# Attention weights split in pieces, with their rest part on GpSimd, and a reordered start of both feed-forward phases

## The chip, the cores and the metric

The kernel runs on one core of one Trainium2 chip. A core has five engines with instruction queues of their own: TensorE (PE: matmuls and transposes into PSUM), VectorE (DVE), ScalarE (ACT), GpSimd (POOL) and SyncE (SP), which here only issues DMA transfers. Each queue is worked off in order; engines wait for each other on semaphores. Time is device time of one execution in microseconds (us), the median of several runs.

## The reference

x has 4 x 512 tokens of 256 values. All is fp32.

```python
x = x + 0.5 * ffn(layernorm(x))
x = x + attention(layernorm(x))      # 16 heads of 128, 4 key/value heads, rope, causal
x = x + 0.5 * ffn(layernorm(x))

def ffn(x):
    logits = x @ router_w + router_b                      # 8 experts
    topk_vals, topk_idx = top_k(logits, 2)
    full_w = one_hot sum of softmax(topk_vals)            # (tokens, 8)
    h = silu(einsum('td,edf->etf', x, expert_w) + expert_b[:, None, :])
    out = einsum('etf,te->tf', h, full_w) @ proj_w + proj_b
    y = x + out
    return norm_w * y / sqrt(mean(y * y) + 1e-6)
```

## The kernel before

Every fp32 matmul is made of three products of parts: an operand is copied by ScalarE into a rounded lead part (`hi`, type fp32r), and the rest part (`lo`) is the operand minus the lead. hi*hi, hi*lo and lo*hi are summed in PSUM. The two parts of the weights are made on the chip as well.

There are three phases: feed-forward f1 (0 to 168 us), attention (168 to 734 us), feed-forward f2 (734 to 867 us). `ffn_phase` makes both f1 (`first` is true) and f2. Every engine's instructions are written in order in a function of its own, with helpers and a `body(i)` for each of four blocks of 512 tokens. A block has 16 units (a pair of experts p = 0..3, half g = 0..1, tile t = 0..1): TensorE's `experts` makes a unit of 128 tokens x 2 experts in one of four PSUM banks (`ex`, used in a ring), ScalarE applies `silu` in place, VectorE's `weighted` adds it, times the router's weight, to `acc` and so frees the bank. Between the units lie the other steps: layer norm of a later block (`norm_stats`, `norm_rows` on VectorE, `rstd` on GpSimd; the rows `z` are transposed by TensorE, `z_lead` and `z_rest` split them), the router (`router`, `logits_out`, `logits_back`, `choose`, `half_tanh`, `weigh_chosen`), and the end of the block before (`sum_T`, `sum_lead`, `sum_rest`, `project`, `add_residual`, `squares`, `mean_square`, `inverse_rms`, `scale_rows`, `add_rows`). f1 also normalises blocks 0 and 1 again, for attention (j = 4 and 5 of `NORMS`).

f1 does more beside its blocks. The expert weights are shifted by a row (`row_of`, a K = 2 matmul of TensorE per pair of experts; `shift_pair` on VectorE for pairs 0 and 1; `row_out` on ScalarE and `shift_late` on GpSimd for pairs 2 and 3) and split (`pair_lead`, `pair_rest`). And the attention weights of four groups, in the order 1, 2, 3, 0, are loaded into `ga` (`a_raw`), their queries scaled by GpSimd (`scale_queries`), split into `gb` (`a_hi`) and `gc` (`a_lo`), and stored to `split` in DRAM, from which the attention phase reads them. Group 0 stays on the chip, in other buffers. A group is split in four pieces of 640 columns: `group_lead` on ScalarE and `group_rest` on VectorE, both at the places that `SLOTS` names (slot 8*i + 4*g + p of the order of units). SyncE's `store_group` waits until all four pieces of a group are split, then issues the load of the next group and two stores. `group_lead` waits for the scaling and, from the second group on, for the stores of the whole group before (semaphore `a_out`), as it overwrites `gb`:

```python
                    act.wait_ge(a_scaled, C * k + C)
                    if k > 0 and (ORDER[k] > 0 or m > 0):
                        act.wait_ge(a_out, 32 * k)
```

The kernel prints below with the line numbers of the profile: `group_lead` is line 623, `group_rest` 420, `silu` 602, `squares` 612, `weighted` 442 and 445, `norm_rows` 358, `pair_rest` 425, `scale_queries` 282, `residual` 265, `shift_late` 273, `row_of` 733, `router` 740 and 741, `experts` 764 to 766, `transpose_z` 719.

## Time and profile before

| | |
|---|---|
| time, median of 3 runs | 867.75 us (866.32 to 869.53) |
| the profiled execution | 870.1 us, its span 867.2 us |
| granted TensorE clock, mean | 0.971 |
| TensorE busy | 803.8 us (93% of the span) |
| VectorE busy | 679.8 us (78%) |
| ScalarE busy | 503.6 us (58%) |
| GpSimd busy | 484.8 us (56%) |
| HBM read and written | 19.77 MB and 11.01 MB, 35 GB/s over the span |

The span runs from the first to the last instruction; some time lies around it. A busy share is an average over three phases with different limits; the rows further below look at single stretches. In them L623 is line 623 of the kernel, "[5.98 <-DMA ...]" means that the engine stood idle for 5.98 us before this instruction and what released it, and PEclk is the clock granted to TensorE, as a share of full speed.

### The profile page before, as it was taken

What the parts mean: (1) busy time and instruction counts of PE and PEld (TensorE: products, weight loads), DVE (VectorE), ACT (ScalarE), POOL (GpSimd) and SP (SyncE); (2) the same over time, 40 slices, a digit from 0 to 9 for tenths busy, and PEclk for the clock granted to TensorE, in tenths of its full rate; (3) what the DMA queues carried; (4) which work ended last, traced back from release to release, by engine and by line L of the source; (5) the groups of instructions that cost most, each with busy time, mean ns of one, the idle gap of its engine ahead of it and who ended that gap; (6) DMA issues with size and microseconds to landing.
All of it is one profiled execution on the core that took longest, in us unless ns stands there. A gap on an engine that the chain in (4) does not pass through costs nothing. (4 is left out here: it accounts for less than half of the span.)

```text
span 867.2 us, 16033 instructions
## 1 busy us (share of the span) xinstructions
PE 803.8 (93%) x4712; PEld 703.5 (81%) x4712; DVE 679.8 (78%) x1948; ACT 503.6 (58%) x1241; POOL 484.8 (56%) x382
## 2 busy tenths in 40 slices
PE   7897897867899999999999999999999998799995
PEld 4676676655799999999998998999999997688884
DVE  6887898599966877868768768768778797888874
ACT  3434544445665766767758558657667674445442
POOL 4312331268577787777877877877877751212211
PEclk9998998979999999999999999999999999899997
DMA  9040451410112312312212212132121100000001
GB/s 306 3 173 16 176 183 48 115 44 13 37 30 69 97 24 48 83 38 73 73 36 58 75 36 73 24 97 49 56 65 30 40 17 1 1 1 25 25 1 49
DMA packets 25238, 52.18 MB, mean 60 GB/s; under 512 B 3442, under 2 KB 9202, under 8 KB 23922
## 3 DMA queue, kind: packets, MB, share of 16 engines
q1 hardware_dynamic: 25204, 51.77, 20.9%
q8 instruction: 16, 0.26, 0.1%
q14 instruction: 18, 0.15, 0.1%
HBM read 19.77 MB, written 11.01 MB: 35 GB/s over the span
## 5 line engine op out<-in xcount | busy, mean ns | idle before, releaser
L1147 DVE TENSOR_TENSOR at_ptl<-at_pt,at_pth 128x512 fp32r<-128x512 f32 (+1 forms) x192 | 108.8, 593 | 45.0 <-ACT at_pth L1293 44.9
L1293 ACT ACTIVATE at_pth<-at_pt 128x512 fp32r<-128x512 f32 (+1 forms) x192 | 94.2, 525 | 85.6 <-PE at_pt L1451 85.6
L1287 ACT ACTIVATE at_pr<-at_pr,at_low 128x512 f32<-128x512 f32 (+3 forms) x256 | 140.5, 557 | 2.3 <-DVE at_low L1133 2.2
L1035 POOL TENSOR_TENSOR at_ql<-at_rot,at_qh 128x512 fp32r<-128x512 f32 x62 | 79.7, 1285 | 98.1 <-ACT at_qh L1272 98.1
L602 ACT ACTIVATE f_ex<-f_ex 128x512 f32<-128x512 f32 x128 | 74.1, 583 | 86.4 <-PE f_ex L766 86.2
L445 DVE SCALAR_TENSOR_TENSOR f_acc<-f_ex,f_full,f_acc 128x256 f32<-128x256 f32 x224 | 95.9, 476 | 33.4 <-ACT f_ex L602 32.7
L1142 DVE TENSOR_SCALAR at_pr<-at_pr,at_inv 128x128 f32<-128x128 f32 (+3 forms) x256 | 110.5, 492 | 2.3
L1050 POOL TENSOR_TENSOR at_rot<-at_rot,gc 128x512 f32<-128x512 f32 x78 | 101.4, 1300 | 8.1 <-POOLq L1067 2.1
L1044 POOL TENSOR_TENSOR at_rot<-ga,cos 128x512 f32<-128x512 f32 x78 | 101.9, 1307 | 4.1 <-POOL at_ql L1035 2.4
L1451 PE MATMUL at_pt<-ident,at_pr 128*128 128x128 f32 x640 | 94.1, 278 | 9.5 <-DVE at_pr L1142 8.6
L1046 POOL TENSOR_TENSOR gc<-gc,sin 128x512 f32<-128x512 f32 x78 | 102.3, 1312 | 0.0
L764 PE MATMUL f_ex<-f_e_hi,zh 128*128 128x512 f32 x224 | 94.4, 421 | 6.5 <-DVE f_e_lo L425 4.4
L1133 DVE CUSTOM_DVE_ANT_0 at_pr<-at_sc,at_mask 128x512 f32<-128x512 f32 (+2 forms) x192 | 100.4, 546 | 0.0
L1272 ACT ACTIVATE at_qh<-at_rot 128x512 fp32r<-128x512 f32 x64 | 40.5, 633 | 92.7 <-POOL at_rot L1050 90.6
L765 PE MATMUL f_ex<-f_e_hi,zl 128*128 128x512 f32 x224 | 91.6, 409 | 0.0
L766 PE MATMUL f_ex<-f_e_lo,zh 128*128 128x512 f32 x224 | 91.1, 406 | 0.0
L1465 PE MATMUL at_o<-at_pth,at_vh 128*128 128x512 f32 (+3 forms) x256 | 82.7, 323 | 0.1
L1467 PE MATMUL at_o<-at_pth,at_vl 128*128 128x512 f32 (+3 forms) x256 | 82.4, 322 | 0.0
L1466 PE MATMUL at_o<-at_ptl,at_vh 128*128 128x512 f32 (+3 forms) x256 | 82.2, 321 | 0.0
L1451 PEld LDWEIGHTS at_pt<-ident,at_pr 128*128 128x128 f32 x640 | 71.2, 142 | 12.4 <-DVE at_pr L1142 9.7
L1440 PE MATMUL at_sc<-at_keys,at_ql 128*128 (+4 forms) x256 | 78.0, 316 | 0.0
L1438 PE MATMUL at_sc<-at_keys,at_qh 128*128 (+3 forms) x192 | 71.3, 371 | 5.4 <-DVE at_ql L1224 5.4
(212 smaller groups left out, 2130.8 us busy)
## 6 DMA issues: line engine op xcount, KB each, us to landing
gc<-ga SPq DMA_DIRECT2D x160, 128.0 KB, 2.3
ga<-in_attn_w SPq DMA_DIRECT2D x4, 1280.0 KB, 7.1
at_wo<-attn_split SPq DMA_DIRECT2D x8, 512.0 KB, 4.1
attn_split<-gb SPq DMA_DIRECT2D x3, 1280.0 KB, 9.8
attn_split<-gc SPq DMA_DIRECT2D x3, 1280.0 KB, 12.4
gb<-attn_split SPq DMA_DIRECT2D x6, 512.0 KB, 4.2
x<-in_x SPq DMA_DIRECT2D x4, 512.0 KB, 9.3
e_raw<-in_expert_w SPq DMA_DIRECT2D x8, 256.0 KB, 6.0
```

The costliest lines, as they stand in the source:

```text
L445: dve.scalar_tensor_tensor(out=acc[:, tile, :], in0=h, scalar=full_w[:, tile, e:e + 1], in1=acc[:, tile, :], op0=ALU.mult, op1=ALU.add).th ...
L764: pe.matmul(o, zh[:, c, tok], hi[:, :, w], start=(c == 0), stop=False)
L765: pe.matmul(o, zl[:, c, tok], hi[:, :, w], start=False, stop=False)
L1044: pool.tensor_tensor(rot[r % 2][:], raw[r], cosT[:], ALU.mult)
L1046: pool.tensor_tensor(swap[r], swap[r], sinT[:], ALU.mult).then_inc(sin_done, 1)
L1050: pool.tensor_tensor(rot[r % 2][:], rot[r % 2][:], swap[r], ALU.add).then_inc(sum_done, 1)
L1133: dve.tensor_tensor_reduce(out=out, in0=sc[bank][:, col:col + w], in1=masked, scale=1.0, scalar=3e38, op0=ALU.add, op1=ALU.min, accum_out= ...
L1142: dve.tensor_scalar(a, a, inv[h % 2][:, i:i + 1], None, ALU.mult).then_inc(nm_done, 1)
L1147: dve.tensor_tensor(ptl[h % 2][:, cols], pt[(NF * h + k) % 2][:, 0:FLEN[k]], pth[h % 2][:, cols].bitcast(F32), ALU.subtract).then_inc(lo_d ...
L1287: act.activation(pr[h % 2][:, cols], pr[h % 2][:, cols], ACT.Exp, bias=low[h % 2][:, i:i + 1], scale=-1.0, accum_out=tot[h % 2][:, i:i + 1 ...
L1293: act.activation(pth[h % 2][:, cols], pt[(NF * h + k) % 2][:, 0:FLEN[k]], ACT.Copy).then_inc(hi_done, 1)
L1451: r = pe.transpose(pt[(NF * h + k) % 2][:, col + (i - kt) * P:col + (i - kt + 1) * P], pr[h % 2][:, OFF[i] + kt * P:OFF[i] + (kt + 1) * P] ...
```

## The change

- A group of attention weights has its four pieces at the columns 0, 768, 1536, 2048 and 2560 (`EDGES`). Load, store and both semaphores (`a_in`, `a_out`) are per piece: SyncE stores a piece as soon as it is split, and then loads the same piece of the next group. `group_lead` waits for its own piece. The last group keeps its layout.
- `SLOTS` moves two pieces of groups 1, 2 and 3 one slot later.
- `group_rest` goes from VectorE to GpSimd, to fixed places in GpSimd's body: two pieces behind `residual` and two at the end.
- Start of f1: on VectorE `norm_rows(0)` comes ahead of `shift_pair(0)`, and `z_rest(0)` ahead of `pair_rest(0)`; the three small operations on constants move from VectorE to GpSimd, ahead of `shift_late`. On ScalarE `z_lead(0)` comes first, and `row_out(3)` behind `logits_out(0)`. On TensorE `row_of(2)` comes behind the first transposes, `row_of(3)` behind the router.
- Start of f2: `pair_rest(2)` comes ahead of `weigh_chosen(0)` (as it already does in f1), and GpSimd's `residual(0)` waits for it.

The diff, with parts that only rename or delete calls cut out:

```diff
--- before.py
+++ after.py
@@ -125,6 +125,10 @@
         w_ps = [ps(f"wide{n}", [P, SEQ]) for n in range(2)]
         t_ps = [ps(f"t{n}", [P, SEQ]) for n in range(2)]
 
+        ORDER = (1, 2, 3, 0)
+        EDGES = (0, QKV, C * QKV, C * QKV + G * D // 2, GW)
+        PIECES = len(EDGES) - 1
+
         rows_in, cols_in = (sem(n) for n in ("rows_in", "cols_in"))
         e_hi_done, e_lo_done, p_hi_done, p_split, r_split, setup, consts = (sem(n) for n in ("e_hi_done", "e_lo_done", "p_hi_done", "p_split", "r_split", "setup", "consts"))
         ln_stats, ln_aggr, ln_var, rstd_done, z_done = (sem(n) for n in ("ln_stats", "ln_aggr", "ln_var", "rstd_done", "z_done"))
@@ -139,7 +143,8 @@
         if first:
             e_in = [sem(f"e_in{n}") for n in range(PAIRS)]
             ident_in, x_in, e_row_in = sem("ident_in"), [sem(f"x_in{n}") for n in range(BATCH)], sem("e_row_in")
-            a_in, a_scaled, a_hi_done, a_lo_done, a_out, wa_in = (sem(n) for n in ("a_in", "a_scaled", "a_hi_done", "a_lo_done", "a_out", "wa_in"))
+            a_in, a_out = ([sem(f"{n}{m}") for m in range(PIECES)] for n in ("a_in", "a_out"))
+            a_scaled, a_hi_done, a_lo_done, wo_out = (sem(n) for n in ("a_scaled", "a_hi_done", "a_lo_done", "wo_out"))
             tables_in, step_done = sem("tables_in"), sem("step_done")
             row_ready, e_shifted, row_done, e_shifted_late = (sem(n) for n in ("row_ready", "e_shifted", "row_done", "e_shifted_late"))
 
@@ -154,9 +159,7 @@
         J0 = 0 if first else 1
         NORMS = BATCH + 2 if first else BATCH
 
-        ORDER = (1, 2, 3, 0)
-        PIECES = 4
-        SLOTS = ((3, 4, 5, 6), (10, 11, 12, 13), (17, 18, 19, 20), (25, 26, 27, 28))
+        SLOTS = ((3, 4, 5, 6), (9, 10, 12, 13), (17, 18, 20, 21), (25, 26, 28, 29))
 
         def piece_at(i, g, p):
 
...
-        def group_piece(i, m):
-
-            if ORDER[i] > 0:
-                part = slice(m * GW // PIECES, (m + 1) * GW // PIECES)
+        def group_piece(k, m):
+
+            if ORDER[k] > 0:
+                part = slice(EDGES[m], EDGES[m + 1])
...
@@ -196,14 +199,15 @@
         def _(sp):
             xr = d["x"].rearrange("(b t p) d -> b p t d", t=BT, p=P)
 
-            def load_group(i):
-                sp.dma_start(a_raw[:], d["attn_w"][ORDER[i]]).then_inc(a_in, 16)
-
-            def store_group(i):
-                sp.wait_ge(a_lo_done, PIECES * (i + 1))
-                load_group(i + 1)
-                sp.dma_start(split[ORDER[i], 0], a_hi[:].bitcast(F32)).then_inc(a_out, 16)
-                sp.dma_start(split[ORDER[i], 1], a_lo[:].bitcast(F32)).then_inc(a_out, 16)
+            def load_piece(k, m):
+                part = slice(EDGES[m], EDGES[m + 1])
+                sp.dma_start(a_raw[:, part], d["attn_w"][ORDER[k]][:, part]).then_inc(a_in[m], 16)
+
+            def store_piece(k, m):
+                part = slice(EDGES[m], EDGES[m + 1])
+                sp.wait_ge(a_lo_done, PIECES * k + m + 1)
+                sp.dma_start(split[ORDER[k], 0][:, part], a_hi[:, part].bitcast(F32)).then_inc(a_out[m], 16)
+                sp.dma_start(split[ORDER[k], 1][:, part], a_lo[:, part].bitcast(F32)).then_inc(a_out[m], 16)
 
             def load_block(b):
@@ -223,17 +227,22 @@
                 load_pair(2)
                 load_pair(3)
                 load_block(1)
-                load_group(0)
+                for m in range(PIECES):
+                    load_piece(0, m)
                 for b in range(2, BATCH):
                     load_block(b)
                 sp.dma_start(cosT[:], d["rope_cos"]).then_inc(tables_in, 16)
                 sp.dma_start(sinT[:], d["rope_sin"]).then_inc(tables_in, 16)
-                for i in range(KV - 1):
-                    store_group(i)
+                for k in range(KV - 1):
+                    for m in range(PIECES):
+                        store_piece(k, m)
+                        load_piece(k + 1, m)
                 sp.wait_ge(a_lo_done, PIECES * KV)
                 for n in range(2):
-                    sp.dma_start(split[0, n, :, C * QKV:GW], a_lo[:, n * G * D:(n + 1) * G * D].bitcast(F32)).then_inc(a_out, 16)
-                sp.wait_ge(a_out, 32 * KV)
+                    sp.dma_start(split[0, n, :, C * QKV:GW], a_lo[:, n * G * D:(n + 1) * G * D].bitcast(F32)).then_inc(wo_out, 16)
+                for m in range(PIECES):
+                    sp.wait_ge(a_out[m], 32 * (KV - 1))
+                sp.wait_ge(wo_out, 32)
                 for r in range(NR):
                     sp.wait_ge(raw_done, r + 1)
                     sp.dma_start(swap[r][0:HD // 2, :], raw[r][HD // 2:HD, :]).then_inc(swap_in[r], 16)
@@ -275,12 +284,18 @@
             def scale_queries(i):
 
                 k = ORDER[i]
-                pool.wait_ge(consts, 2)
-                pool.wait_ge(a_in, 16 * i + 16)
+                if i == 0:
+                    pool.wait_ge(consts, 2)
                 for c in range(C):
                     q = a_raw[:, c * QKV + HD:c * QKV + QKV - HD].rearrange("p (h d) -> p h d", h=G)
+                    pool.wait_ge(a_in[c], 16 * i + 16)
                     pool.tensor_tensor(q, q, kw[:, k * G:(k + 1) * G].unsqueeze(2).to_broadcast([P, G, HD]),
                                        ALU.mult).then_inc(a_scaled, 1)
+
+            def group_rest(k, m):
+                raw_part, hi, lo = group_piece(k, m)
+                pool.wait_ge(a_hi_done, PIECES * k + m + 1)
+                pool.tensor_tensor(lo, raw_part, hi.bitcast(F32), ALU.subtract).then_inc(a_lo_done, 1)
 
             def inverse_rms(i, g):
                 pair = slice(HT * g, HT * (g + 1))
@@ -303,12 +318,18 @@
                     residual(i + 1)
                 if first and i == 0:
                     scale_queries(i)
+                if first:
+                    group_rest(i, 0)
+                    group_rest(i, 1)
                 if i > 0:
                     inverse_rms(i - 1, 1)
                 if i + 2 < NORMS:
                     rstd(i + 2)
                 if i > 0:
                     add_rows(i - 1, 1)
+                if first:
+                    group_rest(i, 2)
+                    group_rest(i, 3)
 
             pool.memset(mhalf[:], -0.5).then_inc(half_set, 1)
             pool.memset(warm[:, 0], 1.0).then_inc(half_set, 1)
@@ -316,9 +337,14 @@
             pool.tensor_tensor(warm[:, 1], warm[:, 0], mhalf[:], ALU.pow).then_inc(half_set, 1)
             if first:
                 rstd(0)
+                pool.wait_ge(rows_in, 16)
+                pool.tensor_tensor(r_off[:], r_bias, r_first, ALU.subtract).then_inc(consts, 1)
+                pool.tensor_scalar(kw, kw, -float(HD) ** -0.5, None, ALU.mult).then_inc(consts, 1)
+                pool.tensor_scalar(n_w, n_w, 0.5, None, ALU.mult).then_inc(consts, 1)
                 shift_late(2)
                 shift_late(3)
-                pool.wait_ge(rows_in, 16)
+            else:
+                pool.wait_ge(e_lo_done, 3)
             residual(0)
             rstd(1)
             for i in range(BATCH):
@@ -411,13 +437,6 @@
                 w = e_raw[:, 2 * p:2 * p + 2, :].rearrange("p e (c d) -> p e c d", c=C)
                 row = row_ps[p][:].rearrange("p (e d) -> p e d", e=2).unsqueeze(2).to_broadcast([P, 2, C, D])
                 dve.tensor_tensor(w, row, w, ALU.add).then_inc(e_shifted, 1)
-
-            def group_rest(i, g, p):
-                piece = piece_at(i, g, p)
-                if piece is not None:
-                    raw_part, hi, lo = group_piece(*piece)
-                    dve.wait_ge(a_hi_done, PIECES * piece[0] + piece[1] + 1)
-                    dve.tensor_tensor(lo, raw_part, hi.bitcast(F32), ALU.subtract).then_inc(a_lo_done, 1)
 
             def pair_rest(p):
                 dve.wait_ge(e_hi_done, p + 1)
...
+                if first and i == 0 and g == 0:
+                    dve.wait_ge(consts, 3)
                 if i > 0:
                     dve.wait_ge(x_done, 2 * (i - 1) + g + 1)
                 for t in range(HT):
@@ -478,12 +499,9 @@
-                        pair_rest(2)
                 elif i + 1 < NORMS:
                     norm_rows(i + 1, (0, 1))
                 weighted(i, 0, 1)
-                group_rest(i, 0, 1)
                 if i == 0:
                     norm_rows(1)
                     pair_rest(3)
@@ -492,7 +510,6 @@
                 weighted(i, 0, 2)
                 if i > 0:
                     add_residual(i - 1, 1)
-                group_rest(i, 0, 2)
                 if i + 1 < NORMS:
                     z_rest(i + 1)
                 weighted(i, 0, 3)
...
@@ -531,27 +544,22 @@
                 dve.memset(r_hl[:].bitcast(F32), 0.0).then_inc(setup, 1)
                 dve.memset(r_h0[:].bitcast(F32), 0.0).then_inc(setup, 1)
                 norm_stats(0)
+                norm_rows(0)
+                shift_pair(0)
                 dve.wait_ge(cols_in, 16)
                 dve.wait_ge(setup, 2)
                 dve.tensor_copy(r_hl[:, :, 0:E], r_raw).then_inc(r_split, 1)
                 dve.tensor_copy(r_h0[:, :, 0:E], r_raw).then_inc(r_split, 1)
                 dve.wait_ge(r_split, 2)
                 dve.tensor_tensor(r_hl[:, :, E:2 * E], r_raw, r_hl[:, :, 0:E].bitcast(F32), ALU.subtract).then_inc(r_split, 1)
-                shift_pair(0)
-                norm_rows(0)
-                pair_rest(0)
                 dve.wait_ge(ident_in, 16)
                 z_rest(0)
+                pair_rest(0)
                 shift_pair(1)
-                dve.wait_ge(rows_in, 16)
-                dve.tensor_tensor(r_off[:], r_bias, r_first, ALU.subtract).then_inc(consts, 1)
-                dve.tensor_scalar(kw, kw, -float(HD) ** -0.5, None, ALU.mult).then_inc(consts, 1)
-                dve.tensor_scalar(n_w, n_w, 0.5, None, ALU.mult).then_inc(consts, 1)
-                dve.wait_ge(consts, 3)
+                dve.wait_ge(consts, 1)
             pair_rest(1)
             choose(0)
-            if first:
-                pair_rest(2)
+            pair_rest(2)
             weigh_chosen(0)
             for i in range(BATCH):
                 body(i)
@@ -617,9 +625,18 @@
                 if piece is not None:
                     k, m = piece
                     raw_part, hi, _ = group_piece(k, m)
-                    act.wait_ge(a_scaled, C * k + C)
-                    if k > 0 and (ORDER[k] > 0 or m > 0):
-                        act.wait_ge(a_out, 32 * k)
+                    if m < C:
+                        act.wait_ge(a_scaled, C * k + (m + 1 if ORDER[k] > 0 else C))
+                    elif ORDER[k] > 0:
+                        act.wait_ge(a_in[m], 16 * k + 16)
+                    elif m == PIECES - 1:
+                        act.wait_ge(a_in[2], 16 * KV)
+                        act.wait_ge(a_in[3], 16 * KV)
+                    if k > 0 and ORDER[k] > 0:
+                        act.wait_ge(a_out[m], 32 * k)
+                    elif ORDER[k] == 0 and m == 1:
+                        for other in range(3):
+                            act.wait_ge(a_out[other], 32 * k)
                     act.activation(hi, raw_part, ACT.Copy).then_inc(a_hi_done, 1)
 
             def step_out(k):
@@ -683,15 +700,14 @@
             act.wait_ge(half_set, 2)
             act.activation(warm[:, 2], warm[:, 0], ACT.Silu).then_inc(half_set, 1)
             if first:
+                z_lead(0)
+                pair_lead(0)
                 row_out(2)
-                pair_lead(0)
-                row_out(3)
-                act.wait_ge(ident_in, 16)
-                z_lead(0)
             else:
                 pair_lead(1)
             logits_out(0)
             if first:
+                row_out(3)
                 pair_lead(1)
             for i in range(BATCH):
                 body(i)
@@ -836,12 +852,15 @@
 
             if first:
                 pe.wait_ge(e_row_in, 16)
-                for p in range(PAIRS):
-                    row_of(p)
+                row_of(0)
+                row_of(1)
                 pe.wait_ge(ident_in, 16)
                 transpose_first_z()
+                row_of(2)
                 pe.wait_ge(r_split, 3)
             router(0)
+            if first:
+                row_of(3)
             experts(0, 0, 0, (0,))
             logits_back(0)
             experts(0, 0, 0, (1,))
```

## Rows read from the trace of the kernel before

**Rows 1.** Stretches: bounds, length, busy us (instructions) by engine, clock, DMA share, GB/s

```profile
0.00:168.00 168.00, 142.52 (x636) 111.73 (x636) 134.96 (x381) 77.20 (x155) 48.12 (x42) 0.95 0.37 124
...
70.00:75.00 5.00, 3.04 (x7) 2.46 (x8) 4.85 (x12) 3.02 (x8) 3.51 (x2) 0.50 0.01 2
75.00:80.00 5.00, 5.00 (x24) 4.07 (x24) 3.13 (x12) 2.31 (x4) 1.51 (x1) 0.83 0.00 0
```

**Rows 2.** Timeline of ScalarE: start, duration, engine, line, operation, operands, idle before

```profile
52.65 0.39 ACT L612 ACTIVATE f_sq<-f_wide 128x256 f32<-128x256 f32 x1 [2.14 <-DVE f_wide L458]
...
89.97 0.39 ACT L612 ACTIVATE f_sq<-f_wide 128x256 f32<-128x256 f32 x1 [1.97 <-DVE f_wide L458]
...
121.93 0.39 ACT L612 ACTIVATE f_sq<-f_wide 128x256 f32<-128x256 f32 x1 [1.37 <-DVE f_wide L458]
...
156.22 0.38 ACT L612 ACTIVATE f_sq<-f_wide 128x256 f32<-128x256 f32 x1
...
770.01 0.39 ACT L612 ACTIVATE f_sq<-f_wide 128x256 f32<-128x256 f32 x1 [0.48 <-DVE f_wide L458]
...
798.27 0.39 ACT L612 ACTIVATE f_sq<-f_wide 128x256 f32<-128x256 f32 x1 [0.48 <-DVE f_wide L458]
```

**Rows 3.** Timeline of ScalarE: first pieces of groups 1 and 2

```profile
66.80 0.74 ACT L623 ACTIVATE gb<-ga 128x640 fp32r<-128x640 f32 x1 [5.98 <-DMA attn_split<-gc]
...
98.54 0.74 ACT L623 ACTIVATE gb<-ga 128x640 fp32r<-128x640 f32 x1 [3.21 <-DMA attn_split<-gc]
```

**Rows 4.** Timeline of SyncE's queue: next load after group 0

```profile
53.37 0.33 SPq L200 DMA_DIRECT2D ga<-in_attn_w  x1
```

**Rows 5.** Timeline of TensorE: a row product, first router, three resumptions after waits

```profile
8.31 1.91 PE L733 MATMUL f_ex<-f_e_row 2*128 2x512 f32 x2
...
14.54 0.77 PE L740 MATMUL f_t<-zh,r_hl 128*128 128x512 f32 x1 [2.19 <-DVE zl L370]
...
71.97 0.80 PE L740 MATMUL f_t<-zh,r_hl 128*128 128x512 f32 x1 [5.12 <-DVE zl L370]
...
146.62 1.97 PE L719 MATMUL f_t<-ident,z 128*128 128x128 f32 x8 [4.60 <-DVE z L358]
...
746.45 0.80 PE L764 MATMUL f_ex<-f_e_hi,zh 128*128 128x512 f32 x1 [4.29 <-DVE f_e_lo L425]
```

**Rows 6.** Instructions of line 420: count, min/median/max ns, times, form

```profile
L420 DVE TENSOR_TENSOR gc<-ga,gb x12: 809/815/1547, 41.5 to 114.0; 128x640 fp32r<-128x640 f32 x12
...
L420 DVE TENSOR_TENSOR gc<-ga,gc x1: 1918/1918/1918, 143.4 to 143.4; 128x1024 fp32r<-128x1024 f32 x1
```

**Rows 7.** Timeline of VectorE in f1

```profile
15.44 1.66 DVE L547 TENSOR_TENSOR r_off<-rows 128x8 f32<-128x8 f32 x1
...
24.67 0.88 DVE L442 TENSOR_SCALAR f_acc<-f_ex,f_full 128x256 f32<-128x256 f32 x2
...
145.19 1.37 DVE L358 TENSOR_SCALAR z<-x,f_mv,f_rs 128x256 f32<-128x256 f32 x4
```

**Rows 8.** Instructions of GpSimd by form: count, busy us, mean ns, idle before

```profile
L1035 POOL TENSOR_TENSOR at_ql<-at_rot,at_qh 128x512 fp32r<-128x512 f32 x62 | 79.7, 1285 | 98.1 <-ACT at_qh L1272 98.1
L265 POOL TENSOR_TENSOR f_zres<-z,rows 128x1024 f32<-128x1024 f32 x8 | 21.8, 2722 | 27.0 <-DVE f_wide L458 23.1 <-DVE z L358 3.9
```

**Rows 9.** Timeline of VectorE beside GpSimd's work

```profile
14.31 1.21 DVE L413 TENSOR_TENSOR e_raw<-f_wide,e_raw 128x1024 f32<-128x1024 f32 x1
...
210.86 3.77 DVE L1105 TENSOR_SCALAR z<-x,at_mv,at_rs 128x256 f32<-128x256 f32 x4
...
736.81 2.11 DVE L425 TENSOR_TENSOR f_e_lo<-e_raw,f_e_hi 128x1024 fp32r<-128x1024 f32 x1 [2.84 <-ACT f_e_hi L597]
```

**Rows 10.** Timeline of GpSimd

```profile
12.39 4.68 POOL L273 TENSOR_TENSOR e_raw<-e_raw,f_shift 128x1024 f32<-128x1024 f32 x2 [4.69 <-DMA e_raw<-in_expert_w]
...
142.92 1.26 POOL L293 TENSOR_TENSOR x<-x,f_y 128x512 f32<-128x512 f32 x1 [1.57 <-DVE f_y L471]
...
735.46 2.38 POOL L265 TENSOR_TENSOR f_zres<-z,rows 128x1024 f32<-128x1024 f32 x1
```

5 lines of the change are left out of this document (removed).

## Prediction

> **What bounds the kernel now.** I read the table of stretches first: TensorE is busy for 93% of the span, and the attention phase, 168 to 734 us, holds most of that. The change does not touch it, so I look at the two feed-forward phases, 0 to 168 us (called f1) and 734 to 867 us (f2). They compute the same on four blocks of tokens; f1 also splits the attention weights (16 pieces) beside it. A marker tells their pace: ScalarE's first square of `squares(i, 0)`, once per block, at 52.65, 89.97, 121.93 and 156.22 us in f1, and at 770.01 and 798.27 in f2 [rows 2]. So f2 needs 28.3 us for a full block. f1 takes 37.3 and 32.0 us for the same in blocks 1 and 2, and 34.3 us in block 3. It loses up to 9.1, 3.7 and 6.0 us against f2's pace; this is what the change can win.
>
> Where the time goes is in ScalarE's own rows. Its first piece of group 1 starts at 66.80 us after 5.98 us of waiting for a store of group 0, and that of group 2 at 98.54 us after 3.21 us [rows 3]. SyncE sends load and store only at 53.37 us, when all four pieces are split [rows 4]. The activations behind the waiting copy are held, so TensorE runs dry: it resumes at 71.97 us after 5.12 us [rows 5], and then at the lower of its two clock levels, 0.50 of full speed up to 75 us and 0.83 in the 5 us after that [rows 1]. Low clock from 71.97 to some 76.6 us costs half of that, 2.2 us. Of block 1's loss 5.1 + 2.2 = 7.3 us are thus the stall, and 1.8 us smaller things.
> In block 3 TensorE waits 4.60 us, until 146.62, for `z` of the second renormalised block [rows 5], which VectorE only starts at 145.19 us [rows 7], behind a piece of the weights of 1.92 us [rows 6].
>
> **Pieces with own semaphores.** Loads and stores of 2 x 768 and 2 x 512 columns leave as each piece is split. Piece 0 of group 0 is split in the middle of block 0, over 10 us before the 53.37 us at which anything leaves today, so its store and the next load are over before ScalarE wants the buffer at 66.80 - 5.98 = 60.8 us. Both waits of rows 3 go: block 1 gains the 7.3 us, block 2 the 3.2 us. The ScalarE copies stay (four per block). Two pieces move a slot later, which costs nothing, as their stores have most of a block. The extra DMA issues are on SyncE's queue, which has nothing else to do here.
>
> **The rest part on GpSimd.** VectorE loses 12 subtractions of 0.82 us (one took 1.55), three smaller ones of 512 columns and one of 1.92 [rows 6]: about 14 us, 3.3 us a block. GpSimd gets them. Its subtraction of 128x512 takes 1.285 us, 2.5 ns per element, and its 128x1024 addition 2.7 us with its locks [rows 8], so 1.9 us for 768 columns, 1.3 for 512 and 2.5 for 1024: 6.4 us a block, 25.6 us in all. GpSimd is busy 48 of 168 us [rows 1], so its own time is covered; what counts is who waits.
> (a) Behind the pieces in GpSimd's queue are `inverse_rms(i-1,1)`, `rstd(i+2)` and `add_rows(i-1,1)`. In blocks 1 and 2 pieces 0 and 1 follow `residual`, so `inverse_rms` comes some 2.5 us later than now; VectorE wants it about 3 us after it is ready now. I price this at 0, with 0.5 us as the upper bound.
> (b) The two engines lock each other out. Four `z` operations of VectorE, 1.37 us when alone [rows 7], took 3.77 us at 210.86 us beside GpSimd's rotations, and a subtraction of 128x1024 took 2.11 us at 736.81 [rows 9], over just when GpSimd's 2.38 us operation from 735.46 is [rows 10]. A VectorE operation that reads PSUM does not suffer: 1.21 us for 128x1024 at 14.31 [rows 9], in the middle of 4.68 us of GpSimd [rows 10]. One collision with a piece cost 0.73 us (1547 against 815 ns [rows 6]). Per block the exposed ones are `mean_square`, the variance, the gap of the router and the row weights: two or three collisions, some 2 us, against 3.3 us removed. The order matters more than the sum: the router chain sits near the end of the block, where VectorE has least slack. I take +1.0 us per block against f2's pace; the bounds are 0 (all in slack) and 2.9 (four collisions of 0.73).
> So blocks 1 and 2 run at 28.3 + 1.0 = 29.3 us: gains of 37.3 - 29.3 = 8.0 and 32.0 - 29.3 = 2.7 us.
>
> The Trainium skill (SBUF — State Buffer, Who interferes with whom) has a rule that speaks against this step: the port pair that VectorE and GpSimd share is an exclusive lock, held for a whole instruction. By that rule, the trace agrees. Were it a sharing of bandwidth instead, collisions would be priced nearer 0 and the sum would come out some 3 us better.
>
> (c) Block 3 is where the lock bites. Its `norm_rows(5)` follows `scale_rows` and `sum_rest`. GpSimd starts `add_rows` right behind `scale_rows` (1.26 us at 142.92 now [rows 10]) and, new, directly behind it pieces 2 (1.3 us) and 3 (2.5 us). One VectorE operation gets in between two of GpSimd's, as the 3.77 us above suggest. So the four `z` operations end about 1.3 + 1.3 + 2.5 + 3 x 0.35 = 6.2 us after `scale_rows`, which itself comes some 1 us earlier. Now they end at 145.19 + 1.37 = 146.56 [rows 7], 3.7 us after 142.9. Net: TensorE's wait grows by 6.2 - 3.7 - 1.0 = 1.5 us. If VectorE gets all four through first, it shrinks by 3 us: the lower bound.
>
> **First block of f1 reordered.** `z` no longer waits for the shift (1.22 us) and the router's split, nor `z_rest` for `pair_rest(0)`: TensorE's router starts some 2.4 us before today's 14.54 us [rows 5]. But two row products (1.91 us for the two matmuls of one [rows 5]) move behind the transposes and behind the router. The last one now stands in front of the experts: +1.7 us, so the experts start 0.7 us earlier. It also feeds `row_out(3)`, then `shift_late(3)` (half of the 4.68 us [rows 10]), which I work out to start at 16.5 instead of 14.7 us, and `residual(0)` behind it (2.4 us, as at 735.46 [rows 10]) ends at 21.2 us or later. The constants leave VectorE, where the first was locked out for 1.66 us at 15.44 [rows 7] and the next still longer; that frees 3.9 us. But `pair_rest(1)`, ready at 17.4 us, meets `shift_late(3)`, and the gap of the router meets `residual(0)`. In order: `pair_rest(1)` to 20.0, gap locked until 22.4, router to 23.3, `pair_rest(2)` to 24.5, weights to 25.5 us, against 24.67 for the first weighted sum now [rows 7]: +0.8 us, bounds -0.8 (no lock met) and +1.7 (GpSimd first each time).
> The rest of block 0 loses four subtractions, nearly all in slack as TensorE is full there. TensorE's low clock, today beside the matmuls that follow `z`, may come earlier, under the wait for `z`, and give back up to 2.5 us. For all of block 0 I take -1.0 us, bounds -3 and +2.5.
>
> **First block of f2.** TensorE stands for 4.29 us until 746.45 [rows 5], for a subtraction that the change puts ahead of the weights. That alone would win 3 us. But `residual(0)` on GpSimd is now released by just this subtraction, and runs over the seven small operations that follow: a lock of 2.4 us [rows 10]. The first sum then frees TensorE 0.7 us before 746.45. I take -0.7 us, bounds -3.5 and +0.5.
>
> **Sum.** -1.0 (block 0) - 8.0 - 2.7 (blocks 1, 2) + 1.5 (block 3) - 0.7 (f2) = -10.9 us; attention 0. The profiled execution took 870.1 us (867.2 of span and 2.9 around it), 2.35 us or 0.3% over the median of the runs shown. The difference is carried over unchanged: 870.1 - 10.9 = 859.2 us for such an execution, 867.75 - 10.9 = 856.9 us as median.
>
> **Rivals.**
> Clean pace: the locks fall in slack, f1 reaches f2's 28.3 us in blocks 1 and 2 (-9.1, -3.7), block 0 and f2 come to their lower bounds (-3, -3.5), block 3 stays: -19.3, 848 us. For it: VectorE idles some 3 us a block in f2. Against: the pieces follow GpSimd's other work without a gap. Chance 0.18.
> The wait is only moved: ScalarE no longer waits for the store, but for the scaling or for a piece that GpSimd finished late, so half of the 10.5 us of stalls stays: 856.9 + 5.2 = about 862 us. For it: all now hangs on GpSimd's order, with waits for four engines in it. Chance 0.14.
> Slower: the lock decides. The pieces hold it for 25.6 us; if all of that falls on VectorE's path in place of 14 us, that is +11.6, with +1.5 in block 3 and +2.5 and +0.5 in the first blocks, against 10.5 of stalls gone: +5.6, 873 us. It decides once more than some 20 us of the 25.6 are on the path. Against it: most of VectorE's time in these blocks goes to operations that read PSUM. Chance 0.06.
> The forecast has 0.62.
>
> **How the numbers follow.** A measurement of this kernel can tell about 0.5% from no change, 4.3 us. Faster by more (below 863.4): the clean pace, nearly all of the forecast, two thirds of the moved wait: 0.85. Slower: its rival, 0.06. Same: the rest, 0.09. The range holds forecast and moved wait and reaches to the clean pace: 848 to 864 us.
>
> **What would show it.** No piece of ScalarE that waits for a store; the markers of f1 near 29 us apart twice; block 3 still with a wait of 5 to 7 us for `z`; VectorE's small operations stretched beside GpSimd's subtractions; in f2 a stretched weight operation near 741 us. The prediction is wrong if the attention phase changes its length, if block 3's wait vanishes, or if the markers stay 32 us or more apart.

## The result: the kernel after, and its profile

On the same chip the kernel after took 854.16 us (median of 4 runs, 851.89 to 855.44) and the kernel before 867.04 us (865.50 to 869.53). The ratio is 0.9846, with an interval of 0.9813 to 0.9879: faster by 12.9 us, or 1.5%. I had predicted 856.9 us, with a range of 848 to 864.

The profiled execution of the kernel after took 854.68 us, 852.8 of it span; that of before had a span of 867.2 us. The profiled execution of before lay about 3 us over its median and that of after only 0.5, so the spans differ by 14.4 us and the medians by 12.9. Below I account for the 14.4.

Stretches of the kernel after (bounds, length, busy time and instructions of PE, PEld, DVE, ACT, POOL, then the granted clock, DMA share, GB/s). They answer [rows 1]; f1 now ends at 157 us:

```profile
0.00:157.00 157.00, 141.01 (x636) 110.65 (x636) 127.08 (x363) 77.71 (x155) 73.22 (x61) 0.96 0.40 133
133.00:136.00 3.00, 0.82 (x4) 0.82 (x5) 3.00 (x5) 0.00 (x0) 1.65 (x1) 0.50 0.17 70
136.00:139.00 3.00, 3.00 (x11) 2.60 (x10) 2.08 (x4) 1.20 (x2) 0.00 (x0) 0.50 0.70 280
```

TensorE does the same 636 instructions in f1, in 157 instead of 168 us. GpSimd goes from 48.1 to 73.2 us there, and VectorE from 135.0 to 127.1. Two stretches at the low clock are left between 20 us and the end of f1: the one shown, in block 3, and one of some 7 us in block 0, from 26.5 us on. Between 34 and 133 us the granted clock is 1.00.

ScalarE in the kernel after, timeline: the markers of blocks 0 to 3 of f1 and of blocks 0 and 1 of f2, answering [rows 2]:

```profile
51.86 0.39 ACT L620 ACTIVATE f_sq<-f_wide 128x256 f32<-128x256 f32 x1 [1.04 <-DVE f_wide L477]
80.17 0.39 ACT L620 ACTIVATE f_sq<-f_wide 128x256 f32<-128x256 f32 x1 [0.64 <-DVE f_wide L477]
108.94 0.39 ACT L620 ACTIVATE f_sq<-f_wide 128x256 f32<-128x256 f32 x1 [1.05 <-DVE f_wide L477]
144.28 0.38 ACT L620 ACTIVATE f_sq<-f_wide 128x256 f32<-128x256 f32 x1
...
756.03 0.38 ACT L620 ACTIVATE f_sq<-f_wide 128x256 f32<-128x256 f32 x1 [0.49 <-DVE f_wide L477]
784.30 0.39 ACT L620 ACTIVATE f_sq<-f_wide 128x256 f32<-128x256 f32 x1 [0.49 <-DVE f_wide L477]
```

The differences between markers carry the rest of this text. The table has them for the two kernels and for all experiments, each from one profiled execution. "Attention" is the time between ScalarE's table loads at its two ends, "f2 start" the time from the second of these to the first marker of f2. The step from the last marker of f1 to attention is 12.8 us in all of them (13.15 in first_start_undone) and blocks 1 to 3 of f2 agree within 0.04 us, so both are left out.

| kernel | block 0 | block 1 | block 2 | block 3 | attention | f2 start | span |
|---|---|---|---|---|---|---|---|
| before | 52.65 | 37.32 | 31.96 | 34.29 | 565.34 | 35.68 | 867.2 |
| after | 51.86 | 28.31 | 28.77 | 35.34 | 564.45 | 34.52 | 852.8 |
| only_pieces | 52.73 | 30.30 | 30.35 | 30.79 | 566.06 | 34.48 | 853.7 |
| pieces_old_slots | 52.85 | 30.07 | 29.72 | 34.29 | 565.63 | 35.47 | 856.7 |
| slots_alone | 52.50 | 38.96 | 33.51 | 32.35 | 565.16 | 35.58 | 868.1 |
| stores_first | 52.89 | 37.79 | 33.89 | 35.70 | 565.75 | 35.59 | 871.6 |
| group_store | 52.21 | 28.34 | 28.70 | 35.67 | 565.82 | 34.53 | 854.9 |
| rest_on_vector | 53.01 | 30.30 | 30.33 | 32.34 | 566.57 | 34.54 | 856.4 |
| small_rest | 51.06 | 28.17 | 28.34 | 30.23 | 566.44 | 34.54 | 848.1 |
| first_start_undone | 50.95 | 28.35 | 28.67 | 36.21 | 565.24 | 34.53 | 853.9 |
| second_start_undone | 51.45 | 28.34 | 28.68 | 35.73 | 565.35 | 35.60 | 855.1 |
| last_rest_waits | 51.64 | 28.34 | 28.68 | 30.52 | 565.78 | 34.56 | 849.5 |
| all_waits | 50.14 | 28.35 | 28.70 | 32.06 | 561.98 | 33.81 | 844.5 |

From before to after: block 0 -0.79, block 1 -9.01, block 2 -3.19, block 3 +1.05, attention -0.89, f2 start -1.16, the tail behind the last marker -0.41, together -14.4 us. How far such a number repeats is read off kernels that do the same in that place: blocks 1 and 2 agree within 0.2 us, the start of f2 within 0.04 us for six kernels of the new order, attention within some 2 us.

ScalarE in the kernel after, its first pieces of groups 1 and 2, answering [rows 3]:

```profile
57.14 0.84 ACT L640 ACTIVATE gb<-ga 128x768 fp32r<-128x768 f32 x1
...
85.49 0.84 ACT L640 ACTIVATE gb<-ga 128x768 fp32r<-128x768 f32 x1
```

Neither has an idle time before it: the 5.98 and 3.21 us are gone. SyncE's queue in the kernel after, where the first piece's first store and the next load leave, answering [rows 4]:

```profile
39.65 0.35 SPq L209 DMA_DIRECT2D attn_split<-gb  x1
...
40.52 0.47 SPq L204 DMA_DIRECT2D ga<-in_attn_w  x1
```

They leave some 13 us before the 53.37 us of the kernel before. TensorE in the kernel after, answering [rows 5]: the first router, then the resumptions in block 0, in block 3 and at the start of f2:

```profile
12.56 0.76 PE L756 MATMUL f_t<-zh,r_hl 128*128 128x512 f32 x1
...
27.38 0.76 PE L780 MATMUL f_ex<-f_e_hi,zh 128*128 128x512 f32 x1 [3.06 <-DVE f_acc L464]
...
135.18 1.97 PE L735 MATMUL f_t<-ident,z 128*128 128x128 f32 x8 [5.72 <-DVE z L384]
...
732.64 0.47 PE L780 MATMUL f_ex<-f_e_hi,zh 128*128 128x512 f32 x1 [3.31 <-DVE f_acc L464]
```

The wait of block 1 (5.12 us until 71.97 in the kernel before) has no counterpart. That of block 3 is still there and has grown from 4.60 to 5.72 us. Its cause stands in VectorE's and GpSimd's timelines of the kernel after, answering [rows 7, 10]:

```profile
130.21 4.91 DVE L384 TENSOR_SCALAR z<-x,f_mv,f_rs 128x256 f32<-128x256 f32 x4
```

```profile
129.78 1.26 POOL L308 TENSOR_TENSOR x<-x,f_y 128x512 f32<-128x512 f32 x1 [1.35 <-DVE f_y L492]
131.00 1.31 POOL L298 TENSOR_TENSOR gb<-ga,gb 128x512 fp32r<-128x512 f32 x1
132.27 2.38 POOL L298 TENSOR_TENSOR gc<-ga,gc 128x1024 fp32r<-128x1024 f32 x1
```

Four scalings that took 1.37 us before [rows 7] now take 4.91. Beside them run GpSimd's addition and, without a gap, the two last remainders, which end at 134.65, half a microsecond before the scalings do at 135.12. Taken one by one, the first three scalings end at 131.19, 132.46 and 134.80, each 0.15 us behind one of GpSimd's three operations.

### The profile page after: what moved, and what is told of

Its sections match the earlier page's. It is cut to its first block and busy times, and to the rows that moved or that the text cites. A ratio compares the mean times of both kernels' runs of the same rounds, so it can differ in the third digit from the quotient of the medians.

```text
span 852.8 us, 16061 instructions
## 1 busy us (share of the span) xinstructions
PE 802.1 (94%) x4712; PEld 702.2 (82%) x4712; DVE 673.2 (79%) x1929; ACT 504.6 (59%) x1241; POOL 509.4 (60%) x401
```

## The experiments

### The pieces alone, and the rest part back on VectorE

Two runs take the remainders (`lo = raw - hi`) away from GpSimd again. The first also puts both phases' starts back into the order of before, so that of the whole change the pieces, their semaphores and the slots are left. The edit of the second:

```
@@ GpSimd, each block @@
-                if first:
-                    group_rest(i, 0)
-                    group_rest(i, 1)
...
@@ VectorE, weighted sums of each block @@
+                group_rest(i, 0, 1)
...
+                group_rest(i, 1, 2)
```

> The kernel after, with the rest part back on VectorE and both reordered starts undone: the pieces with own semaphores alone. My theory (the stalls of ScalarE are the gain): no wait of ScalarE for a store, blocks 1 and 2 of f1 at 28.3 to 29.5 us (37.3 and 32.0 before), 10 to 12 us faster than before, near 856 us. The rival (the relief of VectorE by 14 us is the gain): the markers stay 31 us or more apart, and at most 4 us are won.

> The kernel after, with only the rest part undone (back on VectorE, at the old places). My theory: blocks 1 and 2 within 1 us of the kernel after (28.3 and 28.8 us), block 3 about 1 us shorter than after's 35.3 us, since GpSimd's pieces no longer lock out norm_rows(5): the time within 2 us of after. The rival (relief of VectorE): 8 us or more slower than after.

only_pieces: 856.85 us (855.53 to 857.71) against 868.94 on that chip, a ratio of 0.9868 with an interval of 0.9851 to 0.9884. rest_on_vector: 858.97 us in one run, 4.8 over the kernel after, where I had expected 2 at most. Blocks 1 and 2 take 30.3 us in both, instead of 37.3 and 32.0. The pieces bring 7.0 and 1.6 us there. I had expected 28.3 to 29.5 us, as I gave VectorE's relief nothing: that is a miss. The interval overlaps that of the complete change (0.9813 to 0.9879): rest part and reordered starts together move the whole by no more than the two measurements can tell.

The rest part on GpSimd takes another 2.0 us from block 1 and 1.6 us from block 2 (30.30 to 28.31, 30.35 to 28.77). In only_pieces VectorE is busy for 28.9 of the 30.3 us of block 1, in the kernel after for 25.2 of the 28.3. Block 3 pays it back: 30.79 (only_pieces) or 32.34 us (rest_on_vector) with the remainders on VectorE, 35.34 with them on GpSimd. The two values at the same work differ by the clock, see below.

### Pieces on GpSimd, but almost empty

To see what the locks cost with VectorE's relief kept, small_rest subtracts only 8 columns of each piece or part (and so leaves out most of the remainders; two `memset` of GpSimd at the start, not shown, fill the rest with zeros):

```
+                if len(raw_part.shape) == 3:
+                    raw_part, hi, lo = raw_part[:, :, 0:8], hi[:, :, 0:8], lo[:, :, 0:8]
+                else:
+                    raw_part, hi, lo = raw_part[:, 0:8], hi[:, 0:8], lo[:, 0:8]
                 pool.tensor_tensor(lo, raw_part, hi.bitcast(F32), ALU.subtract).then_inc(a_lo_done, 1)
```

> The kernel after, with each of the 16 subtractions on GpSimd cut to 8 columns (per half where a piece has two); the rest parts of the attention weights are then mostly zero, which leaves the work of every other engine as it is. It measures GpSimd's lock by itself. My theory: blocks 1 and 2 don't move (28.3 and 28.8 us, locks in slack), the wait for z in block 3 falls from 5.7 us to 1 to 2 us and with it the low clock, block 3 at 28 to 31 us instead of 35.3. The rival (the wait of block 3 comes from VectorE's own queue, not from the lock): block 3 within 1.5 us of 35.3 us.

850.92 us in one run. Against the kernel after, blocks 1 and 2 are shorter by 0.14 and 0.43 us (28.17, 28.34), block 0 by 0.8 and block 3 by 5.11 us (30.23). TensorE in small_rest, where it waits for `z` in block 3:

```profile
130.55 1.09 PE L741 MATMUL f_t<-ident,z 128*128 128x128 f32 x8 [2.76 <-DVE z L390]
```

So the locks of GpSimd's subtractions are nearly free in the middle blocks and cost 5 us in block 3, five times the net +1.05 that the comparison with before shows. Of these 5.1 us, 3.0 are the wait (2.76 for 5.72 us; I had expected 1 to 2) and some 2 the low clock, which follows the longer wait and not the shorter one here.

### Is it the lock, and does a wait on GpSimd undo it?

last_rest_waits makes GpSimd finish nothing earlier; it only holds its last two remainders back until VectorE has written `z`:

```
                 if first:
+                    if i == LAST:
+                        pool.wait_ge(z_done, BT * NORMS)
                     group_rest(i, 2)
                     group_rest(i, 3)
```

> The kernel after, with one wait added: in the last block of the first phase GpSimd waits until all rows of norm_rows(5) are written before it takes the last two remainders (the 1280 and 1024 column pieces of group 0). Theory (the lock is what that block pays): the four scalings of norm_rows(5), 4.91 us in the kernel after, go back to 1.4 us, TensorE's wait for z of 5.72 us goes below 2.5 us, and block 3 goes from 35.34 to 30 to 31.5 us, near the 30.23 of the run that left the remainders out; the whole is 4 to 5 us shorter than the kernel after, 849 to 851 us. Rival 1 (VectorE is simply late there, the lock adds only what the slot would have had to spare): block 3 stays at 34.5 us or more and the whole within 1 us of the kernel after, 853 to 855. Rival 2 (a new wait): the remainders end so late that the square root's first transposes, the last weight loads or the residual additions behind them on GpSimd wait; then block 3 is short but what follows it up to the attention's first table load, 12.78 us, is 3 us or more longer.

851.98 us (849.26 to 852.67), 868.29 for before on that chip, ratio 0.981, interval 0.979 to 0.983. Block 3 went from 35.34 to 30.52 us, within the 30 to 31.5 expected. In its timelines of VectorE, TensorE and GpSimd (three views of the kernel last_rest_waits):

```profile
129.93 1.95 DVE L386 TENSOR_SCALAR z<-x,f_mv,f_rs 128x256 f32<-128x256 f32 x4
```

```profile
131.93 1.10 PE L737 MATMUL f_t<-ident,z 128*128 128x128 f32 x8 [2.75 <-DVE z L386]
```

```profile
131.95 1.28 POOL L298 TENSOR_TENSOR gb<-ga,gb 128x512 fp32r<-128x512 f32 x1 [1.20 <-DVE z L386]
133.20 2.40 POOL L298 TENSOR_TENSOR gc<-ga,gc 128x1024 fp32r<-128x1024 f32 x1
```

Counted from the block's marker the remainders start 1.2 us later than in the kernel after (131.95 - 108.66 against 131.00 - 108.94), in the shadow of TensorE's transposes, and take as long as before. The scalings take 1.95 instead of 4.91 us, the rest over 1.37 being GpSimd's addition, which still runs beside the first of them until 130.76. The step behind block 3 stays 12.79 us, so nothing waits for the later remainders. Both rivals fall: VectorE was not simply late, and no new wait appears. Of the 4.8 us some 3 are the shorter wait and the rest the clock, which did not fall in this execution (TensorE's wait is 2.75 us, where I had expected less than 2.5); all_waits, below, has the same wait with a fall and 32.06 us. So the collision costs 3.3 to 4.8 us.

### GpSimd held back in three places

all_waits adds to this edit the same idea for `residual(0)`, which now waits until VectorE has made the weights of the chosen experts (semaphore `gate`), and which in the kernel after runs over the router's small operations in f1 and over the weights in f2:

```
@@ GpSimd, before the blocks @@
                 shift_late(3)
+                pool.wait_ge(gate, GATE)
             else:
-                pool.wait_ge(e_lo_done, 3)
+                pool.wait_ge(gate, GATE)
             residual(0)
```

These are the collisions in the kernel after. The first, with `shift_late(3)`, is not touched by the edit. VectorE in blocks 0 of f1 and f2: the second remainder, the router's gap, the first weighted sum, and in f2 one operation of the weights:

```profile
18.29 2.56 DVE L444 TENSOR_TENSOR f_e_lo<-e_raw,f_e_hi 128x1024 fp32r<-128x1024 f32 x1 [3.52 <-ACT f_e_hi L605]
...
21.62 1.51 DVE L411 TENSOR_TENSOR f_gap<-f_top 128x4 f32<-128x4 f32 x1
...
25.96 0.88 DVE L461 TENSOR_SCALAR f_acc<-f_ex,f_full 128x256 f32<-128x256 f32 x2
...
728.22 2.35 DVE L425 TENSOR_SCALAR f_w<-f_th 128x4 f32<-128x4 f32 x1
```

GpSimd in the kernel after, at the same times:

```profile
17.38 2.38 POOL L282 TENSOR_TENSOR e_raw<-e_raw,f_shift 128x1024 f32<-128x1024 f32 x1 [1.52 <-ACT f_shift L598]
19.72 3.39 POOL L274 TENSOR_TENSOR f_zres<-z,rows 128x1024 f32<-128x1024 f32 x1
...
728.18 2.37 POOL L274 TENSOR_TENSOR f_zres<-z,rows 128x1024 f32<-128x1024 f32 x1 [5.52 <-DVE f_e_lo L444]
```

> The kernel of last_rest_waits, and in both phases GpSimd's residual(0) waits for the gate (the weights of the chosen experts of the first rows, on VectorE) in place of a fixed place (first phase) and of the third remainder (second phase). Theory (each of the three places costs what the lock stretches, and no more): the first weighted sum at 24.9 instead of 25.96 us in the first phase, so the first marker at 50.8 to 51.2 instead of 51.86; in the second phase the weights' operations go from 2.35 back to 0.2 us and the stretch from table load to first marker from 34.5 to 31.5 to 33 us. Together with block 3 that is 846 to 849 us, 0.5 to 1 % below the kernel after. Rival (residual(0) is needed early: the addition behind the first block waits for it, or router and norm behind it on GpSimd come late): the marker of block 0 or of block 1 is 1 to 3 us later in one of the phases and the whole is no better than last_rest_waits, 849 to 852.

847.75 us (846.68 to 850.61), ratio 0.9773, interval 0.9756 to 0.979, which lies below that of the kernel after. It only touches that of last_rest_waits (0.979 to 0.983), on the same chip. It is the fastest complete kernel of this study. But its parts did not come as expected. VectorE in all_waits, the first weighted sum of f1 and the operation of the weights in f2:

```profile
24.43 0.88 DVE L464 TENSOR_SCALAR f_acc<-f_ex,f_full 128x256 f32<-128x256 f32 x2
...
720.73 0.16 DVE L428 TENSOR_SCALAR f_w<-f_th 128x4 f32<-128x4 f32 x1
```

In f1 the first weighted sum is 1.53 us earlier, more than the 1.06 expected, and the marker 1.72 us (50.14). The lock alone does not account for the marker: the granted clock stays at 1.00 over the first 7 us after 26 us here, where in last_rest_waits it is 0.61 and then 0.90 in the two stretches of 3.5 us behind TensorE's wait, and no run separates the two. In f2 the lock is gone as well (0.16 instead of 2.35 us). TensorE resumes 2.2 us earlier after the table load (8.95 instead of 11.13 us), yet the marker comes only 0.7 us earlier. TensorE's timeline in all_waits shows where the rest went:

```profile
722.97 0.47 PE L783 MATMUL f_ex<-f_e_hi,zh 128*128 128x512 f32 x1 [1.12 <-DVE f_acc L467]
...
728.06 1.09 PE L738 MATMUL f_t<-ident,z 128*128 128x128 f32 x8 [2.06 <-DVE z L387]
```

The wait of 3.31 us became one of 1.12 and, three microseconds of matmuls later, one of 2.06 us for the next block's `z`, which in the kernel after cost only 0.51 us. What was saved stands before the next producer. And block 3 took 32.06 instead of the 30.52 us of last_rest_waits, though both have the same wait there; that is the clock, below. Attention was 561.98 us, 3.8 us less than in last_rest_waits, with nothing edited in it, and outside the 564.4 to 566.6 us of all other kernels here. The traces show where it arose, in the first 80 us of the phase. TensorE, then VectorE in last_rest_waits; VectorE in all_waits:

```profile
198.32 1.55 PE L1398 MATMUL at_pj<-ident,z 128*128 128x128 f32 x8 [4.03 <-DVE z L1126]
```

```profile
194.32 3.95 DVE L1126 TENSOR_SCALAR z<-x,at_mv,at_rs 128x256 f32<-128x256 f32 x4
```

```profile
195.31 1.61 DVE L1127 TENSOR_SCALAR z<-x,at_mv,at_rs 128x256 f32<-128x256 f32 x4
```

The same four scalings take 3.95 us beside GpSimd's work in the one and 1.61 in the other, where GpSimd stands still from 195.8 us on and TensorE has no such wait; over the whole phase it stands idle for 15.2 instead of 20.1 us. So the same lock fell differently. What shifted it there is not shown. Of the 5.0 us between the two spans, 1.5 lie in block 0 (the clock's share included) and 0.75 in the start of f2, where the two added waits act; block 3 takes 1.5 back, and the 3.8 in attention and 0.5 in the tail lie where nothing was edited.

### The two starts, undone one at a time

first_start_undone gives f1's start its old order on all engines; the core of it on VectorE:

```
                norm_stats(0)
-                norm_rows(0)
-                shift_pair(0)
                dve.wait_ge(cols_in, 16)
...
+                shift_pair(0)
+                norm_rows(0)
+                pair_rest(0)
                dve.wait_ge(ident_in, 16)
                z_rest(0)
-                pair_rest(0)
```

> The kernel after, with the start of the first phase in the order of the kernel before (TensorE, VectorE, ScalarE and the three small operations back from GpSimd); all else as after. The run that had all pieces but neither reordered start nor remainders on GpSimd had its first marker at 52.73 us, the kernel after has it at 51.86, and the kernel after with the remainders back on VectorE at 53.01. Theory 1 (the reordered start gives nothing, the 0.8 us come from the remainders that left VectorE): first marker at 51.6 to 52.1 us, everything else as in the kernel after, 854 to 855 us. Theory 2 (my prediction's step: the start itself is worth some 0.8 to 1 us): first marker at 52.6 to 53 us, 855 to 856 us. Either way blocks 1 to 3 keep 28.3, 28.8 and 35.3 us within 0.5.

The first marker came at 50.95 us, earlier than either theory said: the reordered start does not give 0.8 to 1 us, it costs 0.9 (51.86), or 0.5 to 1.3, as the four kernels with the new start and all remainders on GpSimd had 51.45 to 52.21. The granted clock is part of the 0.9: over the first 7 us after TensorE's wait the kernel after had 0.50 and 0.64, first_start_undone 0.62 and 0.89. The three others had 0.54 to 0.61 and then 0.90 to 1.00, so their 0.5 to 1.3 us are the fairer comparison. VectorE in first_start_undone:

```profile
20.24 1.22 DVE L441 TENSOR_TENSOR f_e_lo<-e_raw,f_e_hi 128x1024 fp32r<-128x1024 f32 x1
...
25.23 0.88 DVE L458 TENSOR_SCALAR f_acc<-f_ex,f_full 128x256 f32<-128x256 f32 x2
```

The remainder that met `shift_late(3)` for 2.56 us takes 1.22 here, and the first weighted sum is 0.73 us earlier. What made block 0 shorter than before is that four remainders left VectorE (52.73 in only_pieces, 50.95 here). The whole was 856.52 us in one run, since this execution had a block 3 of 36.21 us and 0.8 us more of attention. With 36.21 block 3 lies outside the 0.5 us that I had allowed it.

second_start_undone, the same for f2:

```
-            else:
-                pool.wait_ge(e_lo_done, 3)
             residual(0)
...
+                    if not first:
+                        pair_rest(2)
```

> The kernel after, with the start of the second phase in the order of the kernel before (third remainder of the weights ahead of the choice's weights, residual(0) without its wait). My prediction had this start at -0.7 us (bounds -3.5 to +0.5); measured was -1.16 from the table load to the first marker (35.68 to 34.52), but a run that had it undone showed 34.48 as well. Theory 1 (the reorder is worth nothing: what the order gains, the locked weights' operation of 2.35 us gives back, and the 1.2 us are the state of TensorE's clock or DMA in the one profile of before): 34.3 to 34.7 us, whole within 1 us of the kernel after. Theory 2 (it is worth 0.7 to 1.2 us in this surrounding): 35.2 to 35.7 us.

The start of f2 took 35.60 us, theory 2. Every kernel with the new order has 34.52 to 34.56, and before, slots_alone, stores_first and pieces_old_slots with the old one 35.47 to 35.68. Only only_pieces, at 34.48, stands out, and its stretches say why. Stretches of second_start_undone, then of only_pieces, from about where TensorE resumes (734.45 and 735.14 us):

```profile
734.30:737.30 3.00, 2.85 (x7) 2.28 (x8) 3.00 (x10) 0.00 (x0) 0.97 (x1) 0.50 0.00 0
737.30:740.30 3.00, 3.00 (x10) 2.31 (x9) 1.48 (x2) 0.91 (x2) 2.96 (x1) 0.50 0.02 5
```

```profile
735.00:738.00 3.00, 2.86 (x8) 2.26 (x9) 3.00 (x10) 0.58 (x1) 0.97 (x1) 0.67 0.00 0
738.00:741.00 3.00, 3.00 (x16) 2.49 (x15) 2.07 (x4) 1.21 (x3) 2.97 (x1) 0.76 0.03 5
```

Same order, same wait (4.28 and 4.30 us for the same subtraction), but in the one TensorE then runs 6 us at the low level and in the other only part of them. I had taken only_pieces as a sign that the reorder is worth nothing; it was a lucky clock.

### Does the early departure of the stores matter?

group_store keeps the change, but holds loads and stores back until the whole group is split:

```
                 for k in range(KV - 1):
+                    sp.wait_ge(a_lo_done, PIECES * (k + 1))
                     for m in range(PIECES):
-                        store_piece(k, m)
                         load_piece(k + 1, m)
+                    for m in range(PIECES):
+                        store_piece(k, m)
```

> The kernel after, but SyncE waits until all four pieces of a group are split, and then issues the four loads and the stores. My theory: the waits of ScalarE for the stores come back, 9 us or somewhat more in two waits, with TensorE's low clock behind them, and blocks 1 and 2 take 37 and 32 us or more: 10 us slower than after, near 865 us. The rival (relief of VectorE): under 3 us slower than after.

857.39 us in one run, and blocks 1 and 2 at 28.34 and 28.70 us, the same as in the kernel after. ScalarE in group_store waits for a store, but hardly:

```profile
58.22 0.85 ACT L642 ACTIVATE gb<-ga 128x768 fp32r<-128x768 f32 x1 [0.65 <-DMA attn_split<-gc]
```

I had expected the stalls to come back and some 865 us; that is a miss. Its loads leave only at 50.26 us and its stores from 52.06 on, and still the copy at 58.22 is held for just 0.65 us: it waits for the stores of its own piece alone, of which the second landed at 58.13, while the last piece's landed at 62.73. The 3.1 us by which the transfers leave earlier than in before (50.26 against 53.37) may help too; no run takes them away separately.

stores_first turns the three transfers of the kernel before round:

```
                 sp.wait_ge(a_lo_done, PIECES * (i + 1))
-                load_group(i + 1)
                 sp.dma_start(split[ORDER[i], 0], ...
                 sp.dma_start(split[ORDER[i], 1], ...
+                load_group(i + 1)
```

> The kernel before, with the order of SyncE's three transfers turned round: the two stores of a group (1280 KB each) go out ahead of the load of the next (1280 KB). In the kernel before the three, sent at 53.4 us, landed 7.2, 9.9 and 12.5 us later, and ScalarE's first piece waited 5.98 us for the last store. Theory 1 (the bandwidth decides: the three need some 12.5 us whatever their order, so that the load is now the last, and ScalarE waits for GpSimd's scaling of 2.09 us behind it): no wait for a store at ScalarE's first piece but one of 6 to 9 us for the scaling, block 1 at 37.5 to 40 us against 37.32, block 2 at 32 to 35 against 31.96, the whole 868 to 874. Theory 2 (my prediction's premise, the late departure of the stores behind a load is the cost, and what the pieces bring is mainly that they leave early): the wait shrinks to 3 us or less, block 1 at 34 us or less, the whole 862 to 865.

873.37 us in one run (before: 867.88), blocks 1 and 2 at 37.79 and 33.89: theory 1. ScalarE in stores_first:

```profile
67.44 0.74 ACT L623 ACTIVATE gb<-ga 128x640 fp32r<-128x640 f32 x1 [6.38 <-POOL ga L282]
...
99.73 0.74 ACT L623 ACTIVATE gb<-ga 128x640 fp32r<-128x640 f32 x1 [3.69 <-POOL ga L282]
```

The wait for the store is gone, and one of 6.38 us for the scaling has taken its place, since the load is now last. The three transfers of 1280 KB sent at 53.37 us in before had all landed at 66.72, those sent at 53.61 here at 65.23: 13.4 and 11.6 us for the same bytes. What helps is that a copy waits for its own quarter of them, not in which order they are sent.

### The slots

The two runs differ from only_pieces and from before in one line:

```
-        SLOTS = ((3, 4, 5, 6), (10, 11, 12, 13), (17, 18, 19, 20), (25, 26, 27, 28))
+        SLOTS = ((3, 4, 5, 6), (9, 10, 12, 13), (17, 18, 20, 21), (25, 26, 28, 29))
```

slots_alone makes this edit in before, pieces_old_slots the reverse one in only_pieces.

> The kernel before with one line changed: the slots of the pieces are those of the kernel after, so that of the last group the 640 and 1024 column pieces come a slot later (28 and 29 instead of 27 and 28; in the middle groups one piece a slot earlier and two a slot later). Whole groups and one semaphore for all stores stay. Question: where the 3.5 us of block 3 come from that the run with all pieces and no other edit showed (34.29 to 30.79). Theory 1 (the slot: the 1.92 us piece no longer stands ahead of the four scalings of z): block 3 at 30.5 to 32.5 us here too, blocks 1 and 2 still 37 and 32 within 0.7, the whole 864 to 865.5 us. Theory 2 (the pieces' own semaphores or sizes give it): block 3 stays at 34 us or more and the whole at 867 to 869. As for the clock: if the fall of the granted clock that followed the 4.60 us wait goes as well, 30.8; if the wait is only 3.5 us but the clock still falls, 32.3.

> The kernel of the run with all pieces and no other edit, but with the slots of the kernel before. Theory 1 (the slot gives block 3's gain, the pieces that of blocks 1 and 2): blocks 1 and 2 at 30.3 us within 0.6, block 3 back at 33.5 to 34.5 us, the whole 3 to 4 us above that run, 859.5 to 861. Theory 2 (the pieces give it all): block 3 at 31 us or less, 856 to 857.5.

pieces_old_slots, 858.49 us in one run: block 3 is back at 34.29 us, to the hundredth that of before, with the same wait and the same piece ahead of `z`. TensorE, then VectorE, in pieces_old_slots:

```profile
137.46 1.97 PE L740 MATMUL f_t<-ident,z 128*128 128x128 f32 x8 [4.60 <-DVE z L368]
```

```profile
134.21 1.91 DVE L430 TENSOR_TENSOR gc<-ga,gc 128x1024 fp32r<-128x1024 f32 x1
136.04 1.37 DVE L368 TENSOR_SCALAR z<-x,f_mv,f_rs 128x256 f32<-128x256 f32 x4
```

So the whole difference of block 3 (34.29 to 30.79) comes with the slot alone. Not all of the 3.5 us is the slot's own: TensorE's wait shrinks from 4.60 to 3.48 us, and the clock, which fell in the one, did not in the other. Blocks 1 and 2 are 0.2 and 0.6 us shorter with the old slots, 30.07 and 29.72. slots_alone, 870.60 us in one run (864 to 865.5 expected), has the same wait of 3.48 us, and there the clock fell: block 3 took 32.35 us, the 32.3 that I had expected for that case. So the slot is worth 1.9 us with a fall of the clock and 3.5 without. But blocks 1 and 2 became slower, 38.96 and 33.51 us, where I had expected no change beyond 0.7. ScalarE's first piece of group 1 in slots_alone:

```profile
66.29 0.74 ACT L623 ACTIVATE gb<-ga 128x640 fp32r<-128x640 f32 x1 [8.43 <-DMA attn_split<-gc]
```

The first piece stands one slot earlier (9 for 10), so ScalarE comes to it earlier and is held for 8.43 us instead of 5.98 in front of more activations. The new slots pay only together with the pieces' own semaphores.

### The clock

The column of block 3 has pairs that differ in nothing but the clock. TensorE waits 3.48 us in only_pieces and 3.47 us in rest_on_vector, for the same `z` in the same order. Stretches of block 3, first only_pieces, then rest_on_vector:

```profile
137.40:140.40 3.00, 3.00 (x17) 2.53 (x16) 3.00 (x6) 1.67 (x3) 0.00 (x0) 1.00 0.00 0
140.40:143.40 3.00, 3.00 (x20) 2.69 (x19) 2.64 (x6) 0.58 (x1) 0.00 (x0) 1.00 0.89 348
```

```profile
137.00:140.00 3.00, 2.80 (x11) 2.61 (x12) 3.00 (x7) 1.20 (x2) 0.00 (x0) 0.52 0.00 0
140.00:143.00 3.00, 3.00 (x16) 2.51 (x15) 1.52 (x3) 0.91 (x2) 0.00 (x0) 0.91 0.79 315
```

In the one the granted clock stays at its full level, in the other it falls to the lower one for some 3 us, and the block takes 32.34 instead of 30.79 us. last_rest_waits (30.52) and all_waits (32.06) form the second pair, at 2.75 us of waiting each:

```profile
132.70:135.70 3.00, 3.00 (x16) 2.45 (x15) 2.42 (x5) 1.59 (x3) 2.90 (x2) 1.00 0.00 0
```

```profile
131.20:134.20 3.00, 3.00 (x12) 2.37 (x11) 1.98 (x5) 1.38 (x3) 2.91 (x2) 0.60 0.00 0
```

Both pairs differ by 1.5 us. slots_alone, with a wait of 3.48 us, is a third case with a fall: 0.57 over the 4 us behind the wait. After the waits of 4.59 and 4.60 us (stores_first, before, pieces_old_slots) and 5.72 us (the kernel after, group_store, first_start_undone, second_start_undone) it fell each time. When it fell differed: over the 6 us behind the same wait of 5.72 us the mean clock was 0.66 in the kernel after and 0.50 in first_start_undone, with 35.34 and 36.21 us for the block.

## Why the prediction was right, point by point

The direction, the range and the value held (856.9 against 854.16 us), and so did most of what I said would show it: no piece waits for a store, block 3 waits 5.72 us for `z` (said: 5 to 7), small operations are stretched beside GpSimd's, and f2 has the stretched weights' operation at 728.22 us. By the steps:

**Pieces with own semaphores** (7.3 and 3.2 us). The pieces alone gave 7.0 and 1.6 us. In block 1 the stall and its low clock were sized rightly; of block 2's 3.21 us half was not to be had (2.2 us with the old slots, 1.6 with the new). My reason was wrong in part: I argued from the stores leaving over 10 us earlier, and group_store, without that, is as fast in these blocks. With a wait for each piece alone it is enough that they leave 3.1 us earlier than before; whether less would do is not shown.

**"Two pieces move a slot later, which costs nothing".** True, but I looked for a cost and did not see the gain that the edit has as long as the remainders are on VectorE. The rows were there: TensorE's 4.60 us wait behind the 1.92 us piece [rows 5, 6], which this very edit moves behind `z`. It is worth 1.9 to 3.5 us. In the complete kernel that piece is not on VectorE at all, and term (c) below counts its absence: the 3.7 us of the kernel before hold it and the 6.2 do not. So no term is missing from the sum here.

**The rest part on GpSimd, +1.0 us a block over f2's pace.** Mis-sized: blocks 1 and 2 took 28.31 and 28.77 us, 0.05 and 0.5 over the pace of 28.27. The collisions happen (small_rest: 0.14 and 0.43 us), but in slack. In this place the rival of the clean pace was nearer, though it was wrong on block 0, block 3 and f2. This term is 1.5 us of the difference between forecast and result.

**(c) Block 3, +1.5 us.** Measured +1.05, with TensorE's wait grown by 1.12. The mechanism was the one I described: addition, 512 and 1024 column remainders in a row, one scaling let in at each gap. Removing the collision alone gave 3.3 to 4.8 us back (all_waits, last_rest_waits), so this is shown. That the size came out so near is luck. From the start of GpSimd's addition to the last scaling it took 5.34 us (129.78 to 135.12) where I had 6.2, against 3.64 before; and the addition starts only 0.15 us earlier in the block (20.84 for 20.99 us behind the marker) where I had 1.0. The two errors, of 0.8 and 0.85 us, cancel.

**First block of f1, -1.0 us.** Measured -0.79, with other parts than I thought: the value is luck. TensorE's router started 2.0 us earlier, at 12.56 (said: 2.4). The first weighted sum came at 25.96 (said: 25.5, bounds 23.9 to 26.4), after both collisions that I had listed, in that order. The reorder as such costs 0.5 to 1.3 us. The four subtractions that left VectorE, which I had put "nearly all in slack", give 1.8 (52.73 to 50.95). And the low clock gave nothing back: it was at 0.50 and 0.64 over the 7 us behind TensorE's wait, where before it fell for some 4 us only.

**First block of f2, -0.7 us.** Measured -1.16; undoing it alone costs 1.08. As I said, `residual(0)` locks one of the small operations for 2.35 us. The term was sized too low: TensorE resumes 0.99 us sooner after the table load (11.13 for 12.12 us), where I had 0.7. The last 0.2 us are open. The clock is no ready answer: in last_rest_waits it stood at 0.50 and 0.53 over the first 6 us after the same wait, against 0.59 and 0.85 in the kernel after, and the start of f2 took 34.56 us all the same.

**Attention 0.** It was 0.89 us shorter and the tail 0.41. Executions with the same attention differ by 2 us, so I assign no cause, and do not take it for the sign of being wrong that I had named.

Summed over the profiled executions I had -10.9 and measured -14.4 us: 1.5 from blocks 1 and 2, 0.45 from block 3, 0.5 from f2, 1.3 from attention and tail, less 0.2 in block 0. Of the medians on one chip the difference is -12.9.

**The rivals.** "The wait is only moved" did not happen here, but stores_first is exactly it: the store's wait of 5.98 us turned into 6.38 us for the scaling. "The lock decides" has its mechanism confirmed and its size refuted: of the 25.6 us that GpSimd's pieces hold the lock, some 5 us in block 3, the low clock behind them included, and 1.4 in blocks 0 to 2 were on the path (small_rest against after), far from the 20 that it would have needed.

## What to carry to other kernels

When one engine waits for a set of transfers, give each piece of the buffer its own semaphore and wait for that piece alone: this won 8.6 us in two blocks here, where sending the same bytes in another order won nothing. Work moved to GpSimd should be held back behind VectorE's short chains that TensorE waits for (one more wait on GpSimd won 3.3 to 4.8 us in the block where it mattered), and a slot table should be read against what stands right behind each slot, for gains as well as costs. Work taken off an engine that is busy nearly all the time is worth more than the rows of its waits show: it was 2.0 and 1.6 us here, in blocks whose stalls were already gone. Compare an edit by the block it is in and by more than one profile: TensorE's clock alone made equal blocks differ by 1.5 us.

## What the runs showed of the hardware that I had not expected

The lock between VectorE and GpSimd behaves as if it were granted turn about, so that the number of VectorE's operations counts more than their size. Four scalings beside three GpSimd operations without a gap took 4.91 instead of 1.37 us, one getting in per gap, and one operation of four columns went from 0.17 to 2.35 us, nearly the whole 2.37 us of GpSimd's operation beside it. The Trainium skill (SBUF — State Buffer, Who interferes with whom) calls the shared port pair an exclusive lock held for a whole instruction; the second of these numbers agrees with that. GpSimd pays as well: `residual(0)` from 19.72 took 3.39 us, the first 1.13 of them under VectorE's remainder that ended at 20.85, and 2.39 us in all_waits, where nothing of VectorE stood before it.

The granted clock of TensorE did not follow from the length of the wait before it: after 2.75 us and after 3.48 us of waiting it fell in one trace and not in the other, with the same instructions on both sides. Each fall of some 3 us cost 1.5 us.
